# A graph network's edge stages: gathers that add onto loaded rows, in place of additions on VectorE

## The reference, cut to what matters

```python
h = relu(layernorm(x)); x = x + L0(h, src, dst, edge_weight1, ...)   # two attention layers and an MLP
h = relu(layernorm(x)); x = x + L1(h, src, dst, W, a)                # attention by logits
h = relu(layernorm(x)); x = x + L2(h, node_type, src, dst, ...)      # messages by relation
h = relu(layernorm(x)); x = x + L3(h, src, dst, edge_attr_16, ...)   # third attention layer
```

## Time and profile before

| what | value |
| --- | --- |
| runs, us | 8437.22, 8423.8, 8761.34 |
| median | 8437.22 |
| span of the profiled execution, first to last instruction | 7424.4 |
| VectorE, GpSimd, TensorE, ScalarE busy | 74%, 60%, 54%, 42% |
| DMA packets | 905,932 with 687.05 MB |
| logit block: first gather to last normalisation, about | 3588 to 4126 |
| relation block, about | 5051 to 5692 |
| third attention block, about | 5702 to 6765 |

### The profile page before, as it was taken

The page is one execution under the profiler, slowest core; times in us unless marked ns, Lnnn a source line. Parts: engine busy times, 40 slices in busy tenths (PEclk is TensorE's granted clock), DMA queues, the critical chain, the costliest instruction groups (busy, mean ns, idle before and its releaser), DMA issues. The chain is left out here.

```text
span 7424.4 us, 83618 instructions
## 1 busy us (share of the span) xinstructions
PE 4031.4 (54%) x13024; PEld 2382.1 (32%) x13024; DVE 5518.8 (74%) x17035; ACT 3134.5 (42%) x7470; POOL 4450.3 (60%) x4321
## 2 busy tenths in 40 slices
PE   0002666664666666777100689886886777763000
PEld 0001332332333334666100345673332434332000
DVE  4503899886777776667677899886887888886886
ACT  0002666663333334555455100013554666665555
POOL 2777777775777776555577100005664777774776
PEclk9999677776888886555555889657998666665555
DMA  6002555555333332111698000358885555554554
GB/s 186 3 1 40 98 99 98 98 100 79 85 85 85 86 85 47 38 38 38 101 124 122 15 5 1 97 157 119 155 155 115 111 116 114 113 115 108 165 172 134
DMA packets 905932, 687.05 MB, mean 93 GB/s; under 512 B 595425, under 2 KB 744703, under 8 KB 905181
## 3 DMA queue, kind: packets, MB, share of 16 engines
q1 hardware_dynamic: 517168, 403.39, 20.2%
q0 software_dynamic: 137984, 138.92, 17.5%
q10 hardware_dynamic: 250600, 143.02, 6.4%
HBM read 491.06 MB, written 227.24 MB: 97 GB/s over the span
## 5 line engine op out<-in xcount | busy, mean ns | idle before, releaser
L1793 POOL DMA_INDIRECT f_dg<-t_D,c_at x392 | 379.8, 969 | 1132.0 <-POOLq L179 941.3
L802 POOL DMA_INDIRECT b_xg<-t_H,c_at x784 | 829.3, 1058 | 286.3 <-issue 238.7
L802 POOL DMA_INDIRECT g_xg<-t_D,c_at x784 | 805.6, 1028 | 319.5 <-issue 238.4
L802 POOL DMA_INDIRECT a_xg<-t_XL,c_at x784 | 825.8, 1053 | 250.2 <-issue 238.7
L2181 POOL DMA_INDIRECT out<-n_yo,c_at x392 | 431.0, 1099 | 237.6 <-issue 116.1
L1141 POOL DMA_INDIRECT t_RANK<-m_place,m_at x392 | 384.1, 980 | 315.0 <-DMA m_place<-t_POS 215.2
L440 POOL DMA_INDIRECT t_XL<-su_pos,su_scatx x392 | 389.5, 994 | 243.8 <-DMA t_XL<-in_nodes 124.6
L1326 POOL DMA_INDIRECT l_d<-t_D,l_ix x392 | 403.2, 1029 | 172.7 <-issue 118.9
L938 ACT ACTIVATE a_hn<-a_xg,a_sm 128x64 f32<-128x64 f32 x784 | 269.8, 429 | 395.9 <-DVE a_sm L675 395.0
L1375 ACT ACTIVATE l_hn<-l_xs,l_sm 128x64 f32<-128x64 f32 x784 | 265.0, 426 | 276.8 <-DVE l_sm L675 249.3
L2160 ACT ACTIVATE n_h<-n_x,n_sm 128x64 f32<-128x64 f32 (+1 forms) x800 | 269.4, 426 | 210.0 <-DVE n_sm L675 210.0
(11 more groups left out here) (451 smaller groups left out, 13710.1 us busy)
## 6 DMA issues: line engine op xcount, KB each, us to landing
a_ends<-t_LAST SPq DMA_DIRECT2D x98, 256.0 KB, 4.9
t_XSD<-a_xg SPq DMA_DIRECT2D x98, 256.0 KB
t_H<-a_oE ACTq DMA_DIRECT2D x98, 256.0 KB
b_ends<-t_LAST SPq DMA_DIRECT2D x98, 256.0 KB
l_xb<-t_XSD SPq DMA_DIRECT2D x49, 512.0 KB
f_rl<-t_REL SPq DMA_DIRECT2D x49, 512.0 KB
g_xb<-t_XSD SPq DMA_DIRECT2D x98, 256.0 KB
g_ends<-t_LAST SPq DMA_DIRECT2D x98, 256.0 KB, 3.9
```

The source lines that it names most:

```text
L802: nc.gpsimd.indirect_dma_start(xg[k][:, j, i, :], None, table, bass.IndirectOffsetOnAxis(ap=C["at"][:, i, n * J + j:n * J + j + 1], axis=0 ...
L1793: nc.gpsimd.indirect_dma_start(dg[k][:, u, j, :], None, T["D2"], bass.IndirectOffsetOnAxis(ap=C["at"][:, 0, (2 * n + u) * J + j:(2 * n + u ...
```

## The change

In the three blocks the gathers get compute_op=ALU.add: each gathered row is added onto what stands in its place in SBUF, which is the x row loaded there before. The separate tiles for gathered rows and for sums go. In "g" and "f" VectorE's addition is gone altogether; in "l" it remains for the destination half, whose D1 rows are loaded. GpSimd now waits for the landing of the chunk's loads (s_ld, s_xb), for the first chunks too, and SP's load waits for what last read the buffer: hn in "l" and "f", hn and s_xst in "g". GpSimd no longer waits for these itself. In "a" and "b", which share gat_block with "g", nothing changes (they use bypass).

```diff
 # gat_block, tag "g"
             def stored(n, k, q, old):
                 if old:
-                    hold(sp, S["spturn"], (S["hn"], n - SL + 1))
-                sp.dma_start(xb[k][:, :, :, :], rows(T["XSD"], n).rearrange("p j (s d) -> p j s d", s=2)
+                    hold(sp, S["spturn"], (S["hn"], n - SL + 1), (s_xst[k], NXST * q))
+                sp.dma_start(xg[k][:, :, :, :], rows(T["XSD"], n).rearrange("p j (s d) -> p j s d", s=2)
                              ).then_inc(s_xb[k], 16)
...
                 if old and wide:
                     hold(pool, S["turn"], (S["hT"], n - SL + 1))
+                elif tag == "g":
+                    hold(pool, S["turn"], (s_xb[k], 16 * (q + 1)))
                 elif old:
-                    hold(pool, S["turn"], (S["hn"], n - SL + 1), (s_xst[k], NXST * q))
-                    if tag == "a":
-                        hold(pool, S["turn"], (S["at"], n - SL + 1))
+                    hold(pool, S["turn"], (S["hn"], n - SL + 1), (s_xst[k], NXST * q), (S["at"], n - SL + 1))
...
-                            bass.IndirectOffsetOnAxis(ap=C["at"][:, i, n * J + j:n * J + j + 1], axis=0)
-                            ).then_inc(s_g[k], 16)
+                            bass.IndirectOffsetOnAxis(ap=C["at"][:, i, n * J + j:n * J + j + 1], axis=0),
+                            compute_op=ALU.add if tag == "g" else ALU.bypass).then_inc(s_g[k], 16)
...
-                if tag == "g":
-                    dve.wait_ge(s_xb[k], 16 * (q + 1))
-                    ch1(v.tensor_tensor(xg[k][:, :, :, :], xg[k][:, :, :, :], xb[k][:, :, :, :], ALU.add))
 # logit_block
                 if old:
-                    sp.wait_ge(s_xs, n - SL + 1)
+                    sp.wait_ge(s_hn, n - SL + 1)
...
-                hold(pool, s_turn, (s_ix[k], 16 * (q + 1)))
-                if old:
-                    hold(pool, s_turn, (s_xs, n - SL + 1))
+                hold(pool, s_turn, (s_ix[k], 16 * (q + 1)), (s_ld[k], 32 * (q + 1)))
...
-                        d1[k][:, 0, j, :], None, T["D1"],
-                        bass.IndirectOffsetOnAxis(ap=ix[k][:, j:j + 1], axis=0)).then_inc(s_g[k], 16)
+                        xb[k][:, j, 0, :], None, T["D1"],
+                        bass.IndirectOffsetOnAxis(ap=ix[k][:, j:j + 1], axis=0), compute_op=ALU.add).then_inc(s_g[k], 16)
...
-                v.tensor_tensor(xs[k][:, :, :, :].rearrange("p j s d -> p s j d"), d1[k][:, :, :, :],
-                                xb[k][:, :, :, :].rearrange("p j s d -> p s j d"), ALU.add).then_inc(s_xs, 1)
+                v.tensor_tensor(xb[k][:, :, 1, :], d1[k][:, :, :], xb[k][:, :, 1, :], ALU.add).then_inc(s_xs, 1)
 # relation_block
                 if old:
-                    sp.wait_ge(s_f, n - SL + 1)
+                    sp.wait_ge(s_hn, n - SL + 1)
...
-                if old:
-                    hold(pool, s_turn, (s_xs, n - SL + 1))
+                hold(pool, s_turn, (s_xb[k], 48 * (q + 1)))
...
-                            dg[k][:, u, j, :], None, T["D2"],
+                            xb[k][:, u, j, :], None, T["D2"],
...
+                            compute_op=ALU.add).then_inc(s_g[k], 16)
...
-                if old:
-                    dve.wait_ge(s_hn, n - SL + 1)
-                v.tensor_tensor(xs[k][:, :, :, :], dg[k][:, :, :, :], xb[k][:, :, :, :], ALU.add).then_inc(s_xs, 1)
-                dve.wait_ge(s_xs, n + 1)
```

More of the change, by code:

```diff
@@ L730, in gat_block @@
             bB = m.ps("bankB", [P, 1])
-            xb = [m.sb(f"xb{k}", [P, J, 2, D]) for k in slots]
         bT, bT2, bZ, bX, bS, bD, bO = (m.ps(f"bank{b}", [P, CH]) for b in range(7))
@@ L820, in _ @@
             dve.wait_ge(S["clear"], 1)
-            ch1 = Chain(dve, S["ch1"], 1 + LN_OPS + (tag == "g"))
+            ch1 = Chain(dve, S["ch1"], 1 + LN_OPS)
             chz = Chain(dve, S["chz"], 1)
@@ L1292, in logit_block @@
         ix = [m.sb(f"ix{k}", [P, K], I32) for k in slots]
-        d1 = [m.sb(f"d1{k}", [P, 2, K, D]) for k in slots]
+        d1 = [m.sb(f"d1{k}", [P, K, D]) for k in slots]
         xb = [m.sb(f"xb{k}", [P, K, 2, D]) for k in slots]
-        xs = [m.sb(f"xs{k}", [P, K, 2, D]) for k in slots]
         hn = [m.sb(f"hn{k}", [P, 2, K, D]) for k in slots]
@@ L1312, in load @@
                 if old:
-                    sp.wait_ge(s_xs, n - SL + 1)
+                    sp.wait_ge(s_hn, n - SL + 1)
                 sp.dma_start(xb[k][:, :, :, :], rows_by(T["XSD"], n, K).rearrange("p j (s d) -> p j s d", s=2)
                              ).then_inc(s_ld[k], 16)
-                sp.dma_start(d1[k][:, 1, :, :], rows_by(T["D1"], n, K)).then_inc(s_ld[k], 16)
+                sp.dma_start(d1[k][:, :, :], rows_by(T["D1"], n, K)).then_inc(s_ld[k], 16)
             flow(sp, [(0, load)], total=NB, slots=SL)
@@ L1341, in norm @@
                     dve.wait_ge(s_hn, n - SL + 1)
-                v.tensor_tensor(xs[k][:, :, :, :].rearrange("p j s d -> p s j d"), d1[k][:, :, :, :],
-                                xb[k][:, :, :, :].rearrange("p j s d -> p s j d"), ALU.add).then_inc(s_xs, 1)
+                v.tensor_tensor(xb[k][:, :, 1, :], d1[k][:, :, :], xb[k][:, :, 1, :], ALU.add).then_inc(s_xs, 1)
                 dve.wait_ge(s_xs, n + 1)
-                ch(row_moments(nc, xs[k][:, :, :, :].rearrange("p j s d -> p (j s) d"), bn))
+                ch(row_moments(nc, xb[k][:, :, :, :].rearrange("p j s d -> p (j s) d"), bn))
                 if later(n):
@@ L1374, in normed @@
                 for g in range(2 * K):
-                    last = nc.scalar.activation(hn[k][:, g % 2, g // 2, :], xs[k][:, g // 2, g % 2, :],
+                    last = nc.scalar.activation(hn[k][:, g % 2, g // 2, :], xb[k][:, g // 2, g % 2, :],
                                                 ACT.Relu, bias=sm[:, 5, g:g + 1], scale=sm[:, 4, g:g + 1])
@@ L1731, in relation_block @@
         four, two = range(SL), range(2)
-        dg = [m.sb(f"dg{k}", [P, 2, J, D]) for k in four]
         xb = [m.sb(f"xb{k}", [P, 2, J, D]) for k in four]
         ks = [m.sb(f"ks{k}", [P, 2, J]) for k in four]
-        xs = [m.sb(f"xs{k}", [P, 2, J, D]) for k in four]
         hn = [m.sb(f"hn{k}", [P, 2, J, 2, D]) for k in four]
@@ L1754, in relation_block @@
         s_rl, s_kp, s_d2, s_st = (m.sems(x, 2) for x in "rl kp d2 st".split())
-        s_xs, s_n, s_f, s_hn, s_t, s_h, s_v, s_sel, s_m, s_ag, s_b, s_o, s_ch, s_cho, s_turn, s_end, s_pturn = (
-            m.sem(x) for x in "xs n f hn t h v sel m ag b o ch cho turn end pturn".split())
+        s_n, s_f, s_hn, s_t, s_h, s_v, s_sel, s_m, s_ag, s_b, s_o, s_ch, s_cho, s_turn, s_end, s_pturn = (
+            m.sem(x) for x in "n f hn t h v sel m ag b o ch cho turn end pturn".split())
         block = ctx.enter_context(nc.Block())
@@ L1793, in gather @@
                         nc.gpsimd.indirect_dma_start(
-                            dg[k][:, u, j, :], None, T["D2"],
-                            bass.IndirectOffsetOnAxis(ap=C["at"][:, 0, (2 * n + u) * J + j:(2 * n + u) * J + j + 1], axis=0)
-                            ).then_inc(s_g[k], 16)
+                            xb[k][:, u, j, :], None, T["D2"],
+                            bass.IndirectOffsetOnAxis(ap=C["at"][:, 0, (2 * n + u) * J + j:(2 * n + u) * J + j + 1], axis=0),
+                            compute_op=ALU.add).then_inc(s_g[k], 16)
             flow(pool, [(0, gather)], total=NB, slots=SL, looped=False)
@@ L1813, in norm @@
                 dve.wait_ge(s_xb[k], 48 * (q + 1))
-                if old:
-                    dve.wait_ge(s_hn, n - SL + 1)
-                v.tensor_tensor(xs[k][:, :, :, :], dg[k][:, :, :, :], xb[k][:, :, :, :], ALU.add).then_inc(s_xs, 1)
-                dve.wait_ge(s_xs, n + 1)
-                ch(row_moments(nc, flat(xs[k][:, :, :, :]), bn))
+                ch(row_moments(nc, flat(xb[k][:, :, :, :]), bn))
                 norm_factors(nc, ch, bn, sm, s_n)
@@ L1914, in normed @@
                     for c in two:
-                        last = f(hn[k][:, g // J, g % J, c, :], xs[k][:, g // J, g % J, :], ACT.Relu,
+                        last = f(hn[k][:, g // J, g % J, c, :], xb[k][:, g // J, g % J, :], ACT.Relu,
                                  bias=by_kind[:, c, 1, g:g + 1], scale=by_kind[:, c, 0, g:g + 1])
```

## The result

The changed kernel takes 8660.56 us (median of 4 runs, 8657.59 to 8665.09) against 8467.49 us for the kernel before in the same comparison: ratio 1.0261, 95% interval 1.0224 to 1.0298. It is slower by 2.6%; the forecast was 0.5% faster. One of the four runs of the kernel before, 8761.34 us, was in a slower state and is left out of the ratio; the other three have a median of 8437.22 us, 223 less than the changed kernel.

What follows compares the result with a forecast made beforehand. GpSimd's issuing of gathers was taken to bound the logit and third attention stages, VectorE and TensorE the relation stage. Terms summed to -40.5 us, giving 8397 us (-0.5%) from a median of 8437.2; range 8330 to 9000.

Steps and rivals of the forecast that it cites:

- I take 0: Extra GpSimd time of an adding gather over a plain one, in all three stages: taken as 0, bounds 0 to 0.947 us.
- Rival 1: Adding gathers are dearer on GpSimd, paid in logit and third attention, in relation only above a threshold; 8632 to 9795; chance 0.39.
- p: Rival 1's extra GpSimd price per adding gather, in us; it decides from 0.18, and relation pays from 0.22.
- 11.8: Forecast new relation step in us, 12.3 - 0.5; eight gathers cost time there only beyond it.
- 40.5: Forecast net gain in us over three stages: logit -15 + 3, relation -25 + 5, third attention -12 + 3.5.
- I leave that part alone: The timed median lies 1012.8 us above the profiled span; the forecast carried this difference over unchanged.
- The indirect gain: Fewer VectorE additions slow GpSimd's gathers less: logit -15 us, third attention -12, relation nothing; bounds 0 and -32, -63.
- Waits for loads: Gathers in all three stages now wait for loaded rows; claimed covered, costing nothing in steady state.
- start-up terms: First gathers of each stage wait for loads: logit 3 us, relation 5, third attention 3.5; together +11.5.
- Rivals 2 and 3: 2: DMA engines become the bound, 8468 or 8703, chance 0.07. 3: third stage waits for x rows, 8528, chance 0.03.
- Relation: Relation stage: VectorE and TensorE pace, gathers have room; removing the addition gains 25 us, bounds 0 and 34.

Runs made afterwards that it cites:

- second group: Runs on one chip where the kernel before takes 7421 us: changed kernel, its relation stage alone, third attention stage written out without and with adding gathers.
- e0_before: The kernel before, unchanged, run again on a chip where it takes 8542 us; ratio 1.0011.
- e5_after: The changed kernel, unaltered, run again on the chip where the kernel before takes 7421 us; ratio 1.1079.
- e1_bypass: The changed kernel with plain, overwriting gathers in all three stages, so the x addition is left out, against the kernel before; ratio 0.9954.
- e9: The same edit as e1_bypass, run again on another chip, where the kernel before takes 8547 us; ratio 0.9957.
- e6_half: The kernel before with, in the third attention stage, four of each chunk's eight gathers adding and VectorE adding the other half; ratio 0.9808.
- e10_forms: The changed kernel with six relation-stage gathers per step, adding and plain in three sizes; single run read only for durations: adding costs 0.504, 0.578, 0.589 us more.
- e17_pace_all: The kernel before with a useless 128x200 iota after every gather of first and third attention, logit and relation stages; 7999.16 us, ratio 0.9477.

## Why the prediction was wrong

**The step that failed is "I take 0" for the adding gather.** The term's place was right (1,176 gathers on the path) and its bounds held it (0 to 0.947), but its size is 0.606 us. I argued from gathers and scatters that cost the same whatever they move; none of them adds, so they say nothing of an addition. The Trainium skill's rule, cited against me (GPSIMD Engine Reference, When to use GPSIMD; DMA: Bandwidth & Descriptors, Rules for kernel authors), pointed the right way: the queue's packets went from 16 of 2 KB to 128 of 256 bytes per gather (175,616 more packets over 1,568 gathers is 112 each), and the instruction grew, by something other than bytes. The second read of each row that I drew from the rule does not show: the queue's bytes are the same 138.92 MB.

**Rival 1's formula, with the measured p, gives nearly the whole result where its pace holds.** 1176 x 0.606 = 713; relation 49 x (8 x 1.856 - 11.8) = 149; less 40.5: +822 us. Measured on the chip of the second group: 8224.43 - 7421.03 = +803. By stage: relation 149 - 20 = 129, measured 127; third attention 475 - 8.5 = 466, measured 454; logit 238 - 12 = 226, by subtraction 222. On top of 8437 us the same formula gives 9259, outside the range: that 8660.56 lies inside it is luck.

**"I leave that part alone" was the second mistake.** The 1012.8 us between profile and median were not around the stages but inside them: what lies before the first and after the last instruction is under 2 us in e0_before (span 8579.1, time 8580.87) and in the changed kernel (8655.8, 8657.59). So the first profile's times fit a chip where the kernel takes 7421 us, those of the timed runs one where it takes 8440 to 8550. There the third stage lasts 1437 us instead of the profile's 1043, the logit stage 611 instead of 521 and the first attention stage 1326 instead of 1063, with late instructions in all three. That slack paid most of the bill: stage by stage the changed kernel stands +129, +26 and +53 us above e0_before, together 208, for a loss of 223 us in the timed comparison. Stages outside the three did not move by the change: in e5_after the first attention stage lasts 1067 us.

**The indirect gain** was there and, on the chip of the second group, larger than taken. The excess of the mean gather over its median in e5_after is 1581 - 1552 = 29 ns in the logit and 1599 - 1552 = 47 ns in the third stage, so 11 and 37 us against 32 and 63 of before: -21 (taken -15) and -26 (taken -12). These two differences carry the third stage from 475 - 26 to the 448 us by which it grew. The first trace says where the long gathers stood: of 116 in the third stage that took over 0.1 us more than the median, 33 ran beside an addition of line 830, at 12 us in all, and 83 beside the scan of line 882, at 51 us. So the -12 was right for the additions themselves, and the rest of the -26 is fewer or shorter hits by scans. On the other kind of chip, e1_bypass, which keeps plain gathers, shows the gain in the logit stage alone: the mean stands 19 ns above the median instead of 53 in e0_before (-13 us), in the third stage 45 instead of 43. The inference that the Trainium skill's page SBUF — State Buffer (Who interferes with whom) makes, that a tensor_tensor does not hold up descriptor generation, is not borne out as to the gather's time: each of the 116 ran beside a VectorE instruction with two operands in SBUF. What within the gather is held up is not shown.

**Waits for loads** cost nothing in steady state, as stated: GpSimd has no wait over 0.3 us, its ordinary distance, in the steady part of the logit and third stages of e5_after and of the changed kernel. With plain gathers and late instructions they did cost (e1, e9: logit +27 to +46 us), a case that the prediction did not have. The start-up terms of 3 to 5 us were not measured apart. **Rivals 2 and 3** fall: the share of the gathers' queue went from 17.5% to 14.1% on the one kind of chip (e5_after) and from 12.4% (e0_before) to 12.9% on the other, the DMA share of the logit stage is 0.42 in e5_after and 0.43 in the changed kernel, against 0.84 in the earlier trace rows, and no stage waits for x rows. **Relation**: TensorE and VectorE ceased to be its pace, as rival 1 said for p above 0.22.

What stays open is why instructions come late on one kind of chip only, and what plain gathers issued back to back have to do with it. The runs show that useless work between gathers ends it (9 late at 1.44 us, 0 at 1.60) and that writing out the loop doesn't; they don't show the mechanism. It is not distance alone: e6_half, with four plain gathers in a row at 1.25 us, has none late either. Nor is it the granted clock or the DMA engines: the logit stage has no matmuls and a granted clock of 0.50 on both kinds, and the DMA share there is 0.52 (e0_before, 4100 to 4640 us) against 0.84 in the earlier trace rows. How much of a stage's length the late instructions explain is argued and not shown: those counted in e0_before's third stage add up to 151 us, the stage is 394 us longer. That it goes with the chip rests on five chips, one of them of the faster kind.

## What to carry to other kernels

An operation folded into an engine that sets the pace must be priced on that engine first; here 0.5 to 0.7 us of VectorE per step, hidden in two of the three stages, was traded for 4.8 us of GpSimd. When the profile's span and the timed median lie 14% apart, the profile does not show the execution that is timed: find out inside which stages the difference lies before summing terms, for slack there can swallow costs, as it did here. And issuing at full pace may not be fastest: where dependent short instructions start a microsecond apart for no reason shown, try issuing more slowly.

## What the runs showed of the hardware

- An indirect gather of 128 rows of 256 bytes that adds takes 1.552 us of GpSimd against 0.947 (e5_after, first profile); with rows of 512 bytes 1.536 against 0.947, with 64 rows 1.443 against 0.939 (e10_forms). It moves 128 packets of 256 bytes where the plain one moves 16 of 2048.
- On four of five chips VectorE's short instructions came late in stages whose gathers were all plain and issued 1.25 us apart: 101 times by 0.6 to 3.9 us in the third stage of e0_before, 0 times on the fifth chip. The same kernel took 7421 us on that one and 8441 to 8547 us on the four.
- Every plain gather of the first profile's third stage that took over 0.1 us more than the median of 0.947 ran beside an addition or a scan of VectorE with two operands in SBUF (116 of 784).
- Useless work of 0.31 us after each of 2,352 gathers made the kernel 5.2% faster on one of the four (e17_pace_all).
